# A count matrix built block by block: a running total in PSUM instead of sums added in SBUF

## The reference, cut to what matters

```python
deg = jax.ops.segment_sum(jnp.ones_like(src, dtype=x.dtype), dst, num_segments=n)   # src, dst with a loop n -> n
dinv = jnp.where(deg > 0, jax.lax.rsqrt(jnp.maximum(deg, 1e-12)), 0.0)
norm = dinv[src] * dinv[dst]
h = x @ W
msg = h[src] * norm[:, None]
out = jax.ops.segment_sum(msg, dst, num_segments=n) + b
return jax.nn.relu(out)
```

## Time and profile before

| what | value |
|---|---|
| median of three runs | 3039.4 us (3031.73 to 3045.57) |
| profiled execution, first to last instruction (the only time that its page gives) | 2995.2 us |
| busy: PE, DVE, ACT, POOL | 2491.2, 1641.0, 865.6, 587.7 us |
| first to last matmul of the count loop, start to start | 150.6 to 305.2 us |
| mean TensorE clock granted, as a share of full speed | 0.908 |

### The profile page before, as it was taken

One profiled execution on the slowest core, in us unless ns is written; L12 is line 12 of the kernel. 1 busy time (PEld: TensorE's weight loads), 2 busy tenths in 40 slices (PEclk: granted clock), 3 DMA queues, 4 the chain that ended last, 5 costly groups with the idle time before them and its releaser, 6 DMA issues. The chain is left out here.

```text
span 2995.2 us, 31395 instructions
## 1 busy us (share of the span) xinstructions
PE 2491.2 (83%) x10830; PEld 1584.9 (53%) x10830; DVE 1641.0 (55%) x3721; ACT 865.6 (29%) x1943; POOL 587.7 (20%) x563
## 2 busy tenths in 40 slices
PE   4877974999957999995568999999999879858987
PEld 1344553999954777773443454444554434534443
DVE  9999435222243889885235897718962442431000
ACT  2165110111111767672111465105631100101110
POOL 0000037354502444530110000000000001012221
PEclk9999975999978899997689999999999989779989
DMA  4000436568643555542433553215533120469996
GB/s 132 0 1 1 143 82 183 191 217 270 216 131 100 157 151 155 153 110 91 144 123 135 197 189 112 78 60 170 167 111 124 54 96 2 168 213 346 347 345 218
DMA packets 195418, 440.43 MB, mean 147 GB/s; under 512 B 25163, under 2 KB 45371, under 8 KB 194782
## 3 DMA queue, kind: packets, MB, share of 16 engines
q1 hardware_dynamic: 156942, 344.67, 34.4%
q0 software_dynamic: 38320, 93.76, 12.0%
HBM read 394.21 MB, written 43.93 MB: 146 GB/s over the span
## 5 line engine op out<-in xcount | busy, mean ns | idle before, releaser
L2177 PE MATMUL psum<-x_res,HH 125*128 125x512 f32 (+1 forms) x960 | 351.9, 526 | 19.8 <-DVE x_res L2367 19.8
L2177 PEld LDWEIGHTS psum<-x_res,HH 125*128 125x128 f32 x960 | 181.4, 193 | 179.5 <-issue 156.5
L1154 POOL DMA_INDIRECT recd<-edge_records,edge_slots x160 | 194.4, 1215 | 327.9 <-issue 321.5
L1521 POOL DMA_INDIRECT hg<-HT,srcidx x196 | 191.4, 976 | 260.1 <-PE psum L1642 129.6
L1683 ACT ACTIVATE hg<-hg,ex 128x129 f32<-128x129 f32 x784 | 235.2, 389 | 1.6
L1642 PE MATMUL psum<-hg,Dh 128*125 128x258 f32 x784 | 208.6, 425 | 6.6 <-DVE ACC L1584 4.0
L2167 PE MATMUL psum<-W,XO 128*125 128x512 f32 x480 | 209.0, 596 | 0.0
L2926 PE MATMUL psum<-wd,XN 128*40 128x512 f32 (+1 forms) x704 | 167.6, 635 | 27.7 <-DMA wd<-in_L_ffn_W_down 27.7
L1642 PEld LDWEIGHTS psum<-hg,Dh 128*125 128x125 f32 x784 | 160.7, 210 | 40.5 <-issue 6.6
L1188 PE MATMUL psum<-xgT,w 128*128 128x192 f32 x1024 | 174.7, 330 | 1.8 <-DMA w<-in_L_ffn_w 1.8
L1188 PEld LDWEIGHTS psum<-xgT,w 128*128 128x128 f32 x1024 | 168.0, 192 | 6.2 <-DMA w<-in_L_ffn_w 3.2
(11 more groups left out here) (507 smaller groups left out, 4041.8 us busy)
## 6 DMA issues: line engine op xcount, KB each, us to landing
wd<-in_L_ffn_W_down SPq DMA_DIRECT2D x30, 2560.0 KB
w<-in_L_ffn_w SPq DMA_DIRECT2D x64, 1024.0 KB, 15.0
MK<-CT SPq DMA_DIRECT2D x80, 625.0 KB, 3.8
wu<-in_L_ffn_W_up SPq DMA_DIRECT2D x8, 2730.0 KB, 19.4
rows<-ROWS POOLq DMA_DIRECT2D x24, 625.0 KB, 7.3
w<-in_L_ffn_W SPq DMA_DIRECT2D x18, 512.0 KB
t<-in_L_ffn_tv_W SPq DMA_DIRECT2D x16, 512.0 KB
targets<-DROW SPq DMA_DIRECT2D x49, 128.0 KB, 3.7
```

What stands on the lines that cost most here:

```text
L1154: pool.indirect_dma_start(out=g.recd, out_offset=bass.IndirectOffsetOnAxis(ap=g.posi[:, c:c + 1], axis=0), in_=g.E8[:, c, :], in_offset=No ...
L1521: pool.indirect_dma_start(out=hg[j % RING][:, c, :], out_offset=None, in_=g.HT, in_offset=bass.IndirectOffsetOnAxis(ap=g.srcidx[:, j * CH ...
L2177: return pe.matmul(flat[:, at:at + x1 - x0], HH[:, k, h * DH + c * 128:h * DH + c * 128 + 128], z[n % 4][:, x0:x1], start=(k == 0 and i < ...
```

## The change

The two sets of three banks become one set (banks 4, 5 and 6), which is never restarted: only the first matmul of each bank clears it, so after block j the banks hold the counts of all blocks up to j, over all tiles (each target's position within its tile). ScalarE copies the total to row `blk_tile[j]` of `C` after every block, so the last block of a tile leaves the total up to that tile there. After the loop tile n-1 is subtracted from tile n, from the last tile down to the second. Each tile gets at least one block (the `max` in L463). TensorE's loops change places: a column span is outermost, the chunks within it. The targets' one-hot becomes one VectorE instruction over all four chunks. ScalarE no longer clears `C`. Tiles are transposed from the last to the first, and the degree term is formed ahead of the identity additions.

```diff
-            pe.wait_ge(*one.at(CH * (j + 1)))
-            if j >= 2:
-                pe.wait_ge(*added.at(j - 1))
-            for c in range(CH):
-                for w, (a, b) in enumerate(((0, 512), (512, 1024), (1024, NW))):
-                    ins = pe.matmul(g.PS[0:TP, 3 * u + w, 0:b - a], Dh[u][:, c, :], Sh[u][:, c, a:b],
-                                    start=(c == 0), stop=(c == CH - 1))
-            ins.then_inc(*mm.up())
+            for w, (a, b) in enumerate(SPANS):
+                if j:
+                    pe.wait_ge(*kept.at(3 * (j - 1) + w + 1))
+                for c in range(CH):
+                    if w == 0:
+                        pe.wait_ge(*one.at(CH * j + c + 1))
+                    ins = pe.matmul(g.PS[0:TP, TOTAL + w, 0:b - a], Dh[u][:, c, :], Sh[u][:, c, a:b],
+                                    start=(j + c == 0), stop=True, skip_group_check=True)
+                ins.then_inc(*mm.up())
...
         def dve_onehots(j):
             u = j % 2
+            if j >= 2:
+                dve.wait_ge(*mm.at(3 * (j - 1)))
+            dve.tensor_tensor(Dh[u][:], g.iota_tp[:, None, :].to_broadcast([128, CH, TP]),
+                              order[:, 1, j * CH:(j + 1) * CH, None].to_broadcast([128, CH, TP]),
+                              ALU.is_equal).then_inc(*target_hot.up())
...
-            dve_onehots(0)
             for j in range(NB):
-                if j + 1 < NB:
-                    dve_onehots(j + 1)
-                b = dve.value_load(g.blk_tile[0:1, j:j + 1], min_val=0, max_val=NT - 1)
-                dve.wait_ge(*mm.at(j + 1))
...
-                dve.tensor_tensor(row(C, b), ps, row(C, b), ALU.add).then_inc(*added.up())
-            dve.wait_ge(*added.at(NB))
-            dve.tensor_copy(g.deg[:], C[:, :, N]).then_inc(*v.up())
-            for n in range(NT):
+                dve_onehots(j)
+            dve.wait_ge(*kept.at(3 * NB))
+            dve.tensor_copy(g.deg[:, 0:1], C[:, 0, N:N + 1]).then_inc(*v.up())
+            dve.tensor_tensor(g.deg[:, 1:NT], C[:, 1:NT, N], C[:, 0:NT - 1, N], ALU.subtract).then_inc(*v.up())
+            dve.wait_ge(*v.now())
+            dve.tensor_scalar(di[:], g.deg[:], 1.0, None, ALU.add).then_inc(*degree.up())
+            for n in range(NT - 1, -1, -1):
+                if n:
+                    step(dve.tensor_tensor(C[:, n, 0:N], C[:, n, 0:N], C[:, n - 1, 0:N], ALU.subtract))
...
-        def act_targets(j):
...
+        def act_totals(j):
+
+            b = act.value_load(g.blk_tile[0:1, j:j + 1], min_val=0, max_val=NT - 1)
+            for w, (x0, x1) in enumerate(SPANS):
+                act.wait_ge(*mm.at(3 * j + w + 1))
+                act.activation(row(C, b)[:, x0:x1], g.PS[0:TP, TOTAL + w, 0:x1 - x0], ACT.Copy).then_inc(*kept.up())
```

More of the change, by code:

```diff
@@ L289, in prepare @@
         wld, consts = s.sig("weights_loaded"), s.sig("biases_loaded")
-        padded, attributes, cleared = s.sig("pads_stored"), s.sig("copied"), s.sig("cleared")
+        padded, attributes = s.sig("pads_stored"), s.sig("copied")
         counts, summed = s.sig("counts_ready"), s.sig("counts_summed")
-        evac, one, mm, added = s.sig("rows_made"), s.sig("onehots"), s.sig("summed"), s.sig("added")
+        evac, one, mm, kept = s.sig("rows_made"), s.sig("onehots"), s.sig("summed"), s.sig("added")
         blank, counted, turned = s.sig("zero_rows_stored"), s.sig("counted"), s.sig("turned")
@@ L297, in prepare @@
         sums, taken = s.sig("ct_rows_used"), s.sig("tile_added")
-        distance, target_hot = s.sig("risen"), s.sig("rows")
+        target_hot = s.sig("rows")
         placed, sorted_, made = s.sig("one_placed"), s.sig("ones_sorted"), s.sig("slots_turned")
@@ L304, in prepare @@
         READY, MADE, ONES = 9, 14, 16
+        SPANS, TOTAL = ((0, 512), (512, 1024), (1024, NW)), 4
         def sp_program():
@@ L324, in sp_program @@
             sp.wait_ge(*padded.at(16))
-            sp.wait_ge(*added.at(NB))
+            sp.wait_ge(*mm.at(3 * NB))
             sp.dma_start(we, bcast(W_edge, 128)).then_inc(*consts.up(16))
@@ L382, in pe_counts, with pe_turn @@
             pe.wait_ge(*target_hot.at(j + 1))
-            pe.wait_ge(*one.at(CH * (j + 1)))
-            if j >= 2:
-                pe.wait_ge(*added.at(j - 1))
-            for c in range(CH):
-                for w, (a, b) in enumerate(((0, 512), (512, 1024), (1024, NW))):
-                    ins = pe.matmul(g.PS[0:TP, 3 * u + w, 0:b - a], Dh[u][:, c, :], Sh[u][:, c, a:b],
-                                    start=(c == 0), stop=(c == CH - 1))
-            ins.then_inc(*mm.up())
[L392 to L396, removed]
+            for w, (a, b) in enumerate(SPANS):
[7 more added lines that the diff above has]
+                ins.then_inc(*mm.up())
+        def pe_turn(i):
+            u, n = i % 2, NT - 1 - i
+            pe.wait_ge(*counted.at(i + 1))
+            if i >= 2:
+                pe.wait_ge(*cc.at(3 * (i - 1)))
             for k in range(NT):
@@ L435, in pe_program @@
                 pe_counts(j)
-            for n in range(NT):
-                pe_turn(n)
+            for i in range(NT):
+                pe_turn(i)
             pe_aggregate()
@@ L461, in dve_positions @@
             dve.wait_ge(*summed.at(1))
-            step(dve.tensor_scalar(tot[:], g.PS[0:TP, 5, 0:NT], float(BLK - 1), None, ALU.add))
+            step(dve.tensor_scalar(tot[:], g.PS[0:TP, 5, 0:NT], 1.0, float(BLK - 1), ALU.max, ALU.add))
             step(dve.tensor_copy(toti[:], tot[:]))
@@ L516, in dve_counts @@
             dve.wait_ge(*p.at(ONES))
-            dve_onehots(0)
             for j in range(NB):
-                if j + 1 < NB:
-                    dve_onehots(j + 1)
-                b = dve.value_load(g.blk_tile[0:1, j:j + 1], min_val=0, max_val=NT - 1)
-                dve.wait_ge(*mm.at(j + 1))
[L523 to L527, removed]
-                dve.tensor_tensor(row(C, b), ps, row(C, b), ALU.add).then_inc(*added.up())
-            dve.wait_ge(*added.at(NB))
-            dve.tensor_copy(g.deg[:], C[:, :, N]).then_inc(*v.up())
-            for n in range(NT):
+                dve_onehots(j)
[7 more added lines that the diff above has]
+                    step(dve.tensor_tensor(C[:, n, 0:N], C[:, n, 0:N], C[:, n - 1, 0:N], ALU.subtract))
                 own = C[:, n, n * TP:(n + 1) * TP]
                 dve.tensor_tensor(own, own, g.ident[0:TP, 0:TP], ALU.add).then_inc(*counted.up())
-            dve.wait_ge(*v.now())
-            dve.tensor_scalar(di[:], g.deg[:], 1.0, None, ALU.add).then_inc(*degree.up())
             dve.wait_ge(*root.at(1))
@@ L583, in dve_program @@
             dve_edge_vectors()
-            dve.wait_ge(*made.at(4))
+            dve.wait_ge(*made.at(3))
             for t in range(NT):
@@ L617, in act_program @@
             act.wait_ge(*p.at(READY))
-            act.activation(C[:], none[0:TP, None, 0:1].to_broadcast([TP, NT, NW]), ACT.Copy).then_inc(*cleared.up())
             for k in range(NT):
@@ L623, in act_program @@
             act_take(NT - 1)
-            act.wait_ge(*made.at(3))
+            act.wait_ge(*made.at(2))
             for j in range(NB):
-                act_targets(j)
+                act_totals(j)
             act.wait_ge(*degree.at(1))
             act.activation(di[:], di[:], ACT.Sqrt).then_inc(*root.up())
-            for n in range(NT):
+            for i in range(NT):
+                n = NT - 1 - i
                 for k in range(3):
                     m = min(4, NT - 4 * k)
-                    act.wait_ge(*turned.at(3 * n + k + 1))
+                    act.wait_ge(*turned.at(3 * i + k + 1))
                     act.activation(CT[0:TP, 4 * k:4 * k + m, n * TP:(n + 1) * TP],
-                                   g.PS[0:TP, 3 * (n % 2) + k, 0:m * 128].rearrange("p (a b) -> p a b", b=128)[:, :, 0:TP],
+                                   g.PS[0:TP, 3 * (i % 2) + k, 0:m * 128].rearrange("p (a b) -> p a b", b=128)[:, :, 0:TP],
                                    ACT.Copy).then_inc(*cc.up())
```

2 lines of the change are left out of this document (removed).

## The result

The kernel after takes 2999.1 us (median of four, 2992.66 to 3002.99) against 3035.6 us for the kernel before: ratio 0.9876, 95% interval 0.9862 to 0.9889. Which chip this pair ran on is not known. Run again on a known chip, the second of the experiments, it takes 2969.4 against 3001.0 us, ratio 0.9892 (0.9875 to 0.9908). The forecast was 3002 us, 37.4 less; measured are 36.4 and 31.6 less by the medians. Two executions lie far outside all others, one of the kernel before (3941 us) and one of an experiment (7065 us), and are left out of the ratios.

The account below looks back on a forecast made before the run. VectorE was taken to bound the count loop. Loop -40.8 and tail +3.4 gave -37.4 us, from 3039.4 to 3002 us; the range holding 8 in 10 was 2989 to 3016.

Parts of the forecast that it names:

- VectorE bounds the loop before and after: Count loop: VectorE sets the block, 3.19 us before and 2.40 after; TensorE's 2.13 stays below.
- The comparison at 0.58: Count loop: VectorE's added 500-column comparison costs 0.58 us a block, taken from a later stage's same one-hot.
- The slack of the waits: Count loop: VectorE's new wait is met 0.6 us early; ScalarE's copies cost nothing, with 0.4 to spare.
- start of the loop: Count loop's beginning: TensorE starts at 148.8 us and the third block's buffers are free at 151.1, blocks counted from 151.2.
- Loop: Whole count loop: last copy ends at 266.3 us where the last addition ended at 307.1, -40.8 us.
- The tail: Between loop and aggregation: nine subtractions at a pace of 1.72 us, 18.3 in all against 14.9, +3.4 us.
- Behind the aggregation's start: Aggregation stage: masks begin some 11 us later relative to it, leaving 8 to 9 of VectorE's 19.65 us idle.
- (a): Count loop: the chain of ScalarE's copies becomes the bound, block 2.6 us, 10 us more, 3012; 9 in 100.
- (b): Behind the loop: transposes run at the lower clock, ten taking about 2.5 us, +10 together, 3012; 7 in 100.
- (c): Count loop: TensorE's clock falls to 1.2 GHz, block 4.26 us, time 3094; 2 in 100.
- (d): Count loop: VectorE's instructions no longer overlap, block 2.9 us, 23.5 more, 3026; 4 in 100.
- the 44.2 us "around the span": Whole program: the median of 3039.4 lies 44.2 us above the 2995.2 span, taken as the part around it and unchanged.

Follow-up runs that it names:

- two comparisons: The kernel after with VectorE making the targets' one-hot twice per block, the second waiting for the first: 3031.7 us, ratio 0.9991 to the kernel before.
- three loads: The kernel after with ScalarE loading the tile's number three times per block instead of once: 2997.6 us, ratio 0.9884 to the kernel before.
- before_again: The kernel before, unchanged, run once more against the kernel before: 3035.5 us, ratio 1.0002.

## Why the prediction was right

1. *VectorE bounds the loop before and after.* Shown after from both sides: 0.71 us more work on VectorE made the block 0.71 longer (two comparisons), 0.9 us more on ScalarE's queue made it some 0.05 longer (three loads). Shown before from one: with the comparison on VectorE as well, the block of 3.19 became 3.78, 0.59 longer.
2. *The comparison at 0.58.* Measured 0.59; the block of 2.40 is 2.41. The same shape and the same inputs in a later stage were the right row, although the output's type differs.
3. *The slack of the waits.* VectorE's new wait was met early in all blocks but the third, and TensorE's waits for the copies too. The forecast's start of the loop, 148.8 and 151.2, is 148.78 and 151.14 in the trace. ScalarE's three copies were put too high, at 1.65 us for 0.60 + 0.85 = 1.45, and its idle time so too low, at 0.7 for 0.97; that only adds slack.
4. *Loop.* Forecast -40.8; the last copy ends at 266.85 and not at 266.3, so -40.2. The 0.01 that a block is longer makes 0.5 over 47 blocks. That `C` is no longer cleared brings nothing, as forecast: VectorE's first copy of the sorted slots starts at 144.69 us after and at 144.68 before.
5. *The tail.* Forecast +3.4 from 18.3 us; it was 19.1, +4.3. The pace of 1.72 was 1.69. What was too small is its end, for which I took one tile's transposes and copies. Tile 0 needs no subtraction and so comes right behind tile 1: at the end TensorE and ScalarE have two tiles to do, and from the end of the last identity addition (282.29 + 0.49 = 282.78) to the aggregation pass 3.2 us and not 2.0.

```profile
282.29 0.49 DVE L534 TENSOR_TENSOR C<-C,ident 125x125 f32<-125x125 f32 x2
...
282.63 2.45 PE L399 MATMUL psum<-ident,C 125*125 125x125 f32 x20 [0.34 <-DVE C L534]
```

6. *Behind the aggregation's start.* The prediction left VectorE 8 to 9 us before the first sums; it waited 11.72, so the later masks and edge vectors delayed nothing in this stage:

```profile
320.72 0.75 DVE L586 SCALAR_TENSOR_TENSOR Sh<-psum,dinv,b 125x512 f32<-125x512 f32 x1 [11.72 <-PE psum L413]
```

7. *Rivals.* (a) is excluded by the three loads. (b) came, against the forecast's "the clock is 1.00 in both", but cost nothing. The clock by stretches of 2 us of the transposes, and the forty transposes that begin in the first:

```profile
270.00:272.00 2.00, 1.66 (x10) 1.47 (x10) 1.97 (x3) 1.15 (x3) 0.00 (x0) 0.60 0.46 180
272.00:274.00 2.00, 2.00 (x12) 2.00 (x12) 1.93 (x4) 1.45 (x3) 0.00 (x0) 0.55 0.00 0
274.00:276.00 2.00, 1.90 (x18) 1.71 (x17) 1.97 (x4) 1.96 (x5) 0.00 (x0) 1.00 0.00 0
...
270.77 6.44 PE L399 MATMUL psum<-ident,C 125*125 125x125 f32 x40 [0.34 <-DVE C L534]
```

TensorE had been idle for 2.8 us and then ran one burst of ten transposes. The clock then went to the lower level for some 3.4 us (0.4 and 0.45 of two times 2 us, doubled, since the low level is half) and came back while TensorE ran nothing but transposes. The first of these four tiles, all of it at the lower level, took 2.25 us (270.77 to 273.02), more than VectorE's 1.69 and near the forecast's 2.5. But the low stretch was over within two tiles: four tiles took 6.44, 1.61 each, TensorE caught up, and VectorE's pace stayed at 1.69. What the forecast of +10 had wrong is that the clock would stay low for all ten tiles. The Trainium skill's sentence that transposes don't engage the full clock ("TensorE: Matmul & The Clock Gate", Part 4: PE-mode transpose) is not what this trace shows for its f32 transposes: the granted clock rose to 1.00 in them and stayed there. (c) did not come: the clock is 1.00 through the loop. So the Trainium skill's sentence on short idles between matmul groups (same page, A second HAM failure mode: psum-queue depth-cycling) does not describe this loop either. (d) did not either: VectorE's neighbours overlap as before.

What was wrong without harm: the base. 3002 was the median of before less 37.4, and that difference holds within the interval on either chip; but the 44.2 us "around the span" do not exist. What lies around it is 1.8 us, and most of the rest was a later stage at another pace. That the forecast's 3002 lies within 3 us of the measured 2999.1 is in part luck: the kernel before measured 3039.4 in three runs and 3035.6 with a fourth. Had I multiplied anything by the span, it would have been off.

## What to carry to other kernels

An accumulation that reads and writes the same rows for each block can be left in PSUM as a running total, copied out by another engine and differenced once at the end, as here, where the sums are whole numbers and the difference is exact; the gain is that of the engine relieved only if its other work, and what it takes over, fits, and if the matmul order gives each bank's copy time to finish before its next use. Here three pieces had to come together (total, comparison on VectorE, loop order), and leaving out any one of the three gave back the whole gain. Before handing VectorE's work to an idle GpSimd, measure them side by side; and before subtracting the span of one trace from the median of other runs, compare a stage that neither kernel touches.

## What the runs showed of the hardware

- VectorE slowed down while GpSimd worked beside it: four 1250-column bf16 one-hots took 2.59 in place of 1.82 us beside 1.25 us of GpSimd (500 columns), all of it in one of the four, and an f32 subtraction over 875 columns 1.85 in place of 1.06.
- A VectorE comparison of 500 columns cost 0.34 us with all operands 2 bytes wide and neighbours innermost, one of them repeated over the middle dimension, and 0.59 with f32 inputs, one of them repeated along the innermost dimension. Which of type and layout does it, no run tells.
- A weight load of 125 bf16 columns with a step of four elements lasted 0.193 us, with neighbours 0.136.
- The same unchanged loop ran at 8.6 us a block on one chip and 8.0 on another (412.3 and 382.0 us from the first start to the last of 49, 48 distances). In the trace of `before_again`, on the slower chip, ScalarE waited 103.7 us for releases that the profile names "remote"; on the other chip no such wait is among the longest. Which resource that is stays open.
- The granted clock fell to the lower level for some 3.4 us after 2.8 us without a matmul and one burst of ten transposes; ten f32 transposes of 125 x 125 took 2.25 us there, and 20 took 2.45 at the full clock.
